# Rounding a batch in the quantised layer: the spacing operation on GpSimd, the mask one batch ahead on VectorE

## The reference, cut to what matters

```
def _compute_scale(t):
    amax = jnp.max(jnp.abs(t))
    return FP8_MAX / jnp.maximum(amax, 1e-12)          # FP8_MAX = 448.0

def _quantize_fp8(t, scale):
    return jnp.clip(t * scale, -FP8_MAX, FP8_MAX).astype(jnp.float8_e4m3fn)
...
x_scale = _compute_scale(x2)                           # x2: 1024 x 512, normalised rows
w_scale = _compute_scale(weight)                       # weight: 512 x 512
x_fp8 = _quantize_fp8(x2, x_scale)
w_fp8 = _quantize_fp8(weight.T, w_scale)
out = jnp.matmul(x_fp8.astype(jnp.float32), w_fp8.T.astype(jnp.float32))
out = out * (1.0 / x_scale * (1.0 / w_scale))
```

## Time and profile before

| | |
|---|---|
| median of three runs | 1523.57 us (1520.31 to 1523.79) |
| span of the profiled execution, first to last instruction | 1519.0 us |
| VectorE busy | 1080.1 us, 71% |
| TensorE busy | 1394.3 us, 92% |
| GpSimd busy | 718.3 us, 47% |
| the stage of the quantised layer | 1204.2 to 1245.9 us of the span |

### The profile page before, as it was taken

The page is one execution under the profiler, slowest core; times in us unless marked ns, Lnnn a source line. Parts: engine busy times, 40 slices in busy tenths (PEclk is TensorE's granted clock), DMA queues, the critical chain, the costliest instruction groups (busy, mean ns, idle before and its releaser), DMA issues. The chain is left out here.

```text
span 1519.0 us, 31488 instructions
## 1 busy us (share of the span) xinstructions
PE 1394.3 (92%) x11352; PEld 830.9 (55%) x11352; DVE 1080.1 (71%) x2125; ACT 762.1 (50%) x2476; POOL 718.3 (47%) x748
## 2 busy tenths in 40 slices
PE   5798599997999999887999999999999788889998
PEld 4676244445777777444655555555555335434444
DVE  7997665645666666667989888898877779966212
ACT  4777363222434432347666666666665457655111
POOL 4888551001433434845666666665665306734000
PEclk9999799999999999999999999999999898989999
DMA  7999572215999988766775655655545401546000
GB/s 189 186 174 181 124 171 42 35 35 122 174 195 184 170 142 136 127 144 147 154 150 112 113 115 111 140 109 115 105 79 79 123 3 32 127 84 112 17 12 28
DMA packets 524570, 174.63 MB, mean 115 GB/s; under 512 B 482576, under 2 KB 507600, under 8 KB 524416
## 3 DMA queue, kind: packets, MB, share of 16 engines
q1 hardware_dynamic: 524416, 172.62, 59.0%
HBM read 53.27 MB, written 2.10 MB: 36 GB/s over the span
## 5 line engine op out<-in xcount | busy, mean ns | idle before, releaser
L1946 POOL TENSOR_TENSOR a_q_ss<-a_q_ss,half 128x4 f32<-128x4 f32 x64 | 90.1, 1408 | 167.6 <-DVE a_q_ss L1855 84.0
L67 PE MATMUL bank<-a_wq_hi,xn_pair 128*128 128x512 f16 (+1 forms) x384 | 140.8, 367 | 10.9 <-DVE a_kn L1860 5.2
L1768 ACT ACTIVATE a_probs<-a_masked,a_negmax 128x128 f32<-128x128 f32 x256 | 99.6, 390 | 101.6 <-DVE a_negmax L1826 101.6
L1285 POOL TENSOR_TENSOR a_p_hl<-a_probs,a_p_hl 128x512 f16<-128x512 f32 x64 | 74.3, 1162 | 142.3 <-DVE a_p_hl L1209 142.3
L68 PE MATMUL bank<-a_wq_lo,xn_pair 128*128 128x512 f16 (+1 forms) x384 | 140.5, 366 | 0.0
L69 PE MATMUL bank<-a_wq_hi,xn_pair 128*128 128x512 f16 (+1 forms) x384 | 140.3, 365 | 0.0
L67 PE MATMUL bank<-a_wo_hi,a_o_hi 128*128 128x512 f16 x256 | 97.8, 382 | 4.4 <-DVE x_state L1842 3.5
L68 PE MATMUL bank<-a_wo_lo,a_o_hi 128*128 128x512 f16 x256 | 97.7, 382 | 0.0
L69 PE MATMUL bank<-a_wo_hi,a_o_lo 128*128 128x512 f16 x256 | 97.5, 381 | 0.0
L1961 POOL TENSOR_TENSOR a_normal<-a_probs,a_recip 128x512 f32<-128x512 f32 x64 | 90.2, 1410 | 5.0
L716 POOL TENSOR_TENSOR a_p_hl<-a_probs,a_p_hl 128x512 f16<-128x512 f32 x64 | 78.0, 1230 | 23.6 <-DVE a_p_hl L627 16.7
(11 more groups left out here) (467 smaller groups left out, 5022.4 us busy)
## 6 DMA issues: line engine op xcount, KB each, us to landing
a_no<-in_L_xattn_Wo SPq DMA_DIRECT2D x9, 1024.0 KB, 5.7
a_nq<-in_L_xattn_Wq SPq DMA_DIRECT2D x8, 1024.0 KB, 5.8
a_n_wq<-in_L_xattn_Wq SPq DMA_DIRECT2D x4, 768.0 KB, 5.7
a_n_wo<-in_L_xattn_Wo SPq DMA_DIRECT2D x4, 768.0 KB, 6.1
a_nk<-in_L_xattn_Wk SPq DMA_DIRECT2D x9, 256.0 KB, 3.0
a_nv<-in_L_xattn_Wv SPq DMA_DIRECT2D x9, 256.0 KB, 3.1
f_v_hat<-in_L_ffn_w SPq DMA_DIRECT2D x2, 1152.0 KB, 6.2
x_state<-in_x SPq DMA_DIRECT2D x8, 256.0 KB, 5.2
```

What stands on the lines that cost most here:

```text
L67: pe.matmul(out, lh, rh, start=start, stop=False)
L1285: pool.tensor_tensor(p_hl[s % PN][:, 1, t, :], probs[unit(s, t) % PROBS][:, :, :].rearrange("p h n -> p (h n)"), p_hl[s % PN][:, 0, t, :], ...
L1768: m = act.activation(probs[s % 2][:, h, :], src, ACT.Exp, bias=negmax[s % 2][:, h:h + 1], accum_out=total[s % 2][:, h:h + 1])
L1946: pool.tensor_tensor(r[:, :], r[:, :], K.half[:, 0:n], ALU.pow).then_inc(root_done.sem, 1)
```

## The change

VectorE's rounding of a batch keeps three of its four operations. The mask becomes a function of its own, `powers(b)`; it is called for batch 0 ahead of the batches, and for batch b + 1 at the head of `round_fp8(b)`. The spacing operation goes to GpSimd, in a loop over the eight batches between the identity and the square roots, with two new semaphores: f2_power (mask done, VectorE to GpSimd) and f2_spacing (spacing done, GpSimd to VectorE). The weight's own four operations stay on VectorE. Nothing changes on ScalarE, TensorE or SyncE.

```
+        power_done, spacing_done = Steps(K.sem("f2_power"), batches), Steps(K.sem("f2_spacing"), batches)
...
+                for b in batches:
+                    bits = te[b % 2][:, :].bitcast(F32)
+                    pool.wait_ge(power_done.sem, power_done.count(b))
+                    pool.tensor_scalar(bits, bits, 2.0 ** -6, Q.MAGIC, ALU.max, ALU.mult).then_inc(spacing_done.sem, 1)
...
+                def powers(b):
+                    dve.wait_ge(scaled_done.sem, scaled_done.count(b))
+                    if b >= 2:
+                        dve.wait_ge(q_done.sem, q_done.count(b - 2))
+                    dve.tensor_scalar(te[b % 2][:, :], tw[b % 3][:, :].bitcast(I32), 0x7F800000, None,
+                                      ALU.bitwise_and).then_inc(power_done.sem, 1)
+
                 def round_fp8(b):
                     w, e = tw[b % 3], te[b % 2]
                     bits = e[:, :].bitcast(F32)
-                    dve.wait_ge(scaled_done.sem, scaled_done.count(b))
-                    link(dve.tensor_scalar(e[:, :], w[:, :].bitcast(I32), 0x7F800000, None, ALU.bitwise_and))
-                    link(dve.tensor_scalar(bits, bits, 2.0 ** -6, Q.MAGIC, ALU.max, ALU.mult))
+                    if b + 1 < B:
+                        powers(b + 1)
+                    dve.wait_ge(spacing_done.sem, spacing_done.count(b))
                     link(dve.scalar_tensor_tensor(w[:, :], w[:, :], -Q.FP8_MAX, bits, ALU.max, ALU.add))
...
                 link(dve.tensor_scalar(bits, bits, 2.0 ** -6, Q.MAGIC, ALU.max, ALU.mult))
+                powers(0)
                 round_fp8(0)
```

## The result

The changed kernel is slower by 0.27%: the ratio of the times is 1.0027, with a 95% interval of 1.0018 to 1.0036. On a kernel of 1520 us that is 4.1 us (2.7 to 5.5). The medians of 20 runs each are 1525.22 us (1521.42 to 1526.83) against 1520.12, which is 5.1 us apart; the means are 4.0 us apart. With a spread of 5 to 7 us from run to run the total can't say more than the interval does. The three runs of the kernel before that were known at first had a median of 1523.57, which lay near the upper end of the 20 (1517.13 to 1523.79); the forecast of 1529.0 carried these 3.5 us with it. Set on the median of the 20, the forecast +5.4 would have been 1525.5.

The account below looks back on a forecast made before the run. TensorE was taken to bound the stage's middle and VectorE its tail. A loop of +3.3 us plus a hold of 2.15 gave +5.4 on the median 1523.57: 1529.0 us, range 1525.0 to 1533.0.

Parts of the forecast that it names:

- the sum +3.3 + 2.15: Whole change: +3.3 us from the three-engine loop plus 2.15 us from L2821 waiting for GpSimd, +5.4 us in all.
- the hold of L2821 behind GpSimd: L2821 in rounds 2 to 6 waits while GpSimd's spacing goes first: 0.43 us each, 2.15 us in all.
- The bound of the stage: TensorE bounds the middle at 3.08 us per batch, VectorE the last two batches; the end follows L2821 of batch 7.
- The loop that the moved mask closes: Through VectorE, TensorE and ScalarE, once per batch from batch 2: 3.49 us against 3.08 in the middle, +3.3 us.
- VectorE waits for GpSimd behind L2818: GpSimd stands ready when L2818 ends and goes first; L2821 waits, losing 0.43 us in each of five rounds.
- one waits for the other's whole operation: Read from L549 and L712 in an earlier stage: VectorE's two-input operation and GpSimd's exclude each other for the whole operation.
- the price of 0.72 us: Estimated length of GpSimd's spacing, from the nearest rows: the CAST of 0.61 us plus 0.11 for f32 output.
- the 1.3 us that the prediction itself named as a sign of being wrong: For GpSimd's spacing operation: the prediction is wrong if it takes over 1.3 us.
- The beginning is hidden: Batches 0 and 1: delays of roughly 0.5 us at L2818(0) and another 0.5 before L2821(0) vanish under TensorE's spectra.
- The estimate that the time would be over 0.3% longer: Total time: slower by over 0.3%, 4.6 us, chance 0.55; within it 0.42, faster 0.03.
- a likeliest case of +5.4: Loop with hold in the batches: +4.9 to +6.5 us, chance 0.52, own range 1528.0 to 1530.5 us.

Follow-up runs that it names:

- the kernel where GpSimd doesn't hold VectorE up: Changed kernel, but GpSimd sets a 128 x 2048 scratch tile to a constant and the spacing is left out: 1526.98 us, one run, against 1522.04 for the kernel before.
- earlier rows: ScalarE writes the scaled rows one batch earlier, with four tw tiles: ratio to the kernel before 0.9987 with the change, 0.9982 without it.
- GpSimd's scratch operations: Kernel before plus eight operations on scratch tiles in GpSimd's idle stretch, beside VectorE's work: 23.91 us from batch 0's transposes to the last operation, against 23.71.

## Where the prediction held, and the step that failed

The direction and the mechanism came true: the moved mask closes the loop, and VectorE's last operation is held up in each round. The step that failed is the second term of the sum +3.3 + 2.15, the hold of L2821 behind GpSimd. It was put at 0.43 us in each of five rounds and measured 0.29.

- **The bound of the stage.** Right. TensorE's loop sets the pace up to batch 5, and VectorE the tail. The stage's end follows L2821 of batch 7: +4.88 of the stage from there, and the tail behind it kept its length (4.51 us from this operation to the normalisations, before and after).
- **The loop that the moved mask closes.** Right, in place and size: 3.49 per batch forecast, 3.48 in the kernel where GpSimd doesn't hold VectorE up, and +3.20 us for a forecast of +3.3. With earlier rows, which take it out of the pace, the change costs 0.77 us instead of 4.88.
- **VectorE waits for GpSimd behind L2818.** Right in place, wrong in size: this is the step that failed, "one waits for the other's whole operation", with the price of 0.72 us. The spacing takes 1.92 us, beyond the upper end of 1.26 that the nearest rows gave, and beyond the 1.3 us that the prediction itself named as a sign of being wrong. By "the whole operation" VectorE would then have lost 1.6 us in each of five rounds, and the sum would have been over +11. It lost 0.29: L2833 takes 0.98 and ends 0.77 us before GpSimd does. Two errors went against each other, and the term, forecast as 2.15 us, measured 5 x 0.29 = 1.45. That the sum came so near is luck in this term. Why the loss is 0.29 stays open. The Trainium skill's sentence ("SBUF — State Buffer", section "Who interferes with whom"), by which the later one stands still for the other's whole instruction, holds for the two-tensor operation of the earlier trace rows and not for this one. What it says of a GpSimd operation that only writes, that it does not contend, agrees with the set of 1.80 us, beside which VectorE's operation kept its 0.69.
- **The late spacing of batch 7.** Missed. At 2.29 us it ends at 1246.39 and L2830 starts at 1246.42, about 0.2 us later than add alone would let it. So 3.20 + 1.45 + 0.2 = 4.85, for 4.88 measured.
- **The beginning is hidden.** Right, with less room than thought. VectorE idles 1.84 us for the first spacing, xq(0) ends at 1216.74 + 0.98 = 1217.72, and its transposes follow at 1218.56, still at TensorE's own pace. But xq(0) was forecast near 1215.7 in the times of the first trace. Counted from the stage's first operation it is ready after 12.44 us, and with the early rise of the clock in the first trace of before TensorE would have come to it after 12.45: nothing is left of the room.
- **The estimate that the time would be over 0.3% longer** (0.55, against 0.42 for within it) leaned on a likeliest case of +5.4. The stage gave +4.9 and the runs 0.27%, 4.1 us, just within; their interval of 0.18 to 0.36% reaches over the bound. The margin between the likeliest case and the bound was 0.8 us, about as much as the 0.7 by which the hold was missed.
- **The absolute time.** 1529.0 for a measured median of 1525.22: of the 3.8 us, 3.5 are the base of three runs.

## What to carry to other kernels

An instruction that is brought forward in a list brings its wait with it. Ask what produces its input, and whether that producer hangs on what now stands behind it; if it does, a loop is closed, and its sum of steps is the new pace. Take the producer one step earlier first: here a fourth buffer and an earlier scaling gave 0.18% (0.06 to 0.30) with no other change, and the moved mask and spacing gave nothing on top of them. And a price on GpSimd is to be measured for the very pair of steps; here the neighbours in the trace gave 0.72 us for what takes 1.92.

## What the runs showed of the hardware that was not expected

- GpSimd's two-step operation over 128 x 512 f32 takes 0.62 us for sum and product, 1.96 for maximum and product; a single step takes 1.5, longer than the pair of sum and product.
- A VectorE operation with two SBUF inputs (0.69 us alone) that meets GpSimd's slow operation (1.92 us) loses 0.29 us, and GpSimd 0.37; against a two-tensor operation of GpSimd (1.15 us) it had lost 0.73. Operations with one input lost 0.28 to 0.43 beside GpSimd's scratch operations. It looks as if GpSimd keeps VectorE out only for a part of the slow operation; that is a guess, and which part was not tried.
- The moment at which the granted clock rises from 0.50 to 1.00 after the quiet beginning of the stage differs between executions. The transposes of batch 0 came 12.45 and 13.52 us after the stage's first operation in two traces of the kernel before, and 13.28 and 13.39 in two of the change. Spans of single traces can't carry a comparison of this size; distances between two operations inside the stage repeated to 0.01 us.
